# Exact buffers for the probability tiles of a head, GpSimd's running sums gathered in one stretch, the squares of q on ScalarE

## The chip, the cores and the metric

One NeuronCore of a Trainium2 chip runs the whole program. The metric is the device time of one execution in microseconds. All numbers below come from timed runs of the kernel and from one profiled execution of it.

## The reference

A transformer block on x of 2 x 1024 x 256, float32. First attention with 16 heads of 128 (only the part that matters here is shown), then a layer norm over x plus its output, then a mixture of 32 experts with a shared expert, and another layer norm.

```python
q = rmsnorm(q, q_norm_w); k = rmsnorm(k, k_norm_w)      # over the 128 of a head
q = apply_rope(q, cos, sin); k = apply_rope(k, cos, sin)   # the angle depends on the head's index only
scores = jnp.einsum('bhtd,bhsd->bhts', q, k) * scale
scores = 50 * jnp.tanh(scores / 50)
scores = jnp.where(causal_mask, -jnp.inf, scores)
attn = jax.nn.softmax(scores, axis=-1)
out = jnp.einsum('bhts,bhsd->bhtd', attn, v)
return out @ wo.T
```

## The kernel before

**Tiling.** Attention runs in 32 steps `s = 2h + b`, one for each head `h` and batch `b`. In a step the keys of the batch are cut into 8 tiles `j` of 128; tile j holds the transposed probabilities of its 128 keys (partitions) for the queries from 128 j on (columns), so it is 1024, 896, ... 128 columns wide. Float32 accuracy comes from splitting each operand into a "hi" part (rounded to the matmul's format) and a "lo" part (the rest), and from three matmuls hi·hi, lo·hi, hi·lo for each product (`mm3`, L357 to L359). The hi part is made by ScalarE (`copy_hi`, L666), the lo part by VectorE (`lo_of`, L987: source minus hi); q and the weights are split by VectorE alone (a CAST at L997, then the lo).

**A tile's way.** TensorE makes the scores in PSUM; ScalarE takes tanh into `praw` (L699) and exp in place (L705); GpSimd zeroes the upper triangle of the first 128 columns (`mask`, L857); ScalarE makes `prob_hi`, VectorE `prob_lo`; TensorE multiplies with v (`values`). GpSimd also adds every tile to a running sum `pacc` (`accumulate`, L868 and L872), whose column sums TensorE forms with a matmul against ones (`sums`, L391) and which VectorE turns, inverts and uses in the output projection's accumulation (`out_projected`, L1063). Below, "tile j" is VectorE's lo of tile j, and "values j" TensorE's products with it.

**The step's other work.** While a step's scores and values run, the next step's q, k and v are projected, in units that go through two PSUM banks in turn: each unit's matmuls wait until the unit two before has been read out (`open_unit`, semaphore `pj_free`). The order of the units is written out in `UNIT_ORDER` and repeated by hand in the `step` function of each engine: q0, q1, k0, k1 (halves of 512 queries or keys), sums (the column sums of the step before), ss (sums of squares of q and k), four units op0 to op3 of the output projection of the step before, with v0 and v1 between. TensorE's order in a step s (its scores are of s, values 3 to 7 and sums of s-1, the projections for s+1): q0, q1, values 3, scores 0, k0, values 4, k1, scores 1, values 5 to 7, sums, ss, scores 2, scores 3, op0, scores 4, op1, scores 5, v0, op2, values 0 (of s), op3, v1, values 1, scores 6, scores 7, values 2.

**1/rms.** GpSimd squares q (L835) into `qsq`. TensorE sums squares over the head's 128 entries with ones, VectorE turns the result (L1023) into `var`, GpSimd takes the power -1/2 for q (L840) and for k (L843). The one of k is a per-partition scale of the tanh. The one of q must lie along the columns: SP writes it to DRAM (L295) and reads it back as a broadcast to 128 partitions, `rqB` (L297); then VectorE scales q by it (`scale_raw`, L1040) and splits q into `qhat` (cast, lo), which scores 0 of the next step waits for.

**Buffers.** `praw` and `prob` are rings of four tiles of 1024 columns; tanh of tile j waits until tile j-4 has its lo and is added up, and prob_hi of tile j until values j-4 are done. GpSimd's order in a step: masks 6 and 7 and adds 6 and 7 of the step before, squares of q, masks 0 and 1, power for q, adds 0 and 1, masks 2 and 3, add 2, power for k, add 3, and then mask and add of tiles 4 and 5. VectorE's order: (b = 1: split of wo), q0 and q1 out of PSUM, tiles 4 to 7 of the step before, k0 and k1, oT, sums, ss, (b = 0: split of the next q and k weights), op0, tile 0, op1, tile 1, v0, op2, tile 2, op3, scale_raw, tile 3, v1, qhat.

## Time and profile before

| | |
|---|---|
| median of 3 runs | 1169.97 us (1167.75 to 1170.66) |
| the profiled execution | 1168.05 us, its span 1166.3 us |
| busy share of the span: TensorE / VectorE / ScalarE / GpSimd | 88% / 79% / 59% / 68% |
| attention | from the start to about 950 us; the rest is routing and experts |

A busy share is an average over stages; what sets the time of a stage is read from what its engines wait for. A matmul's shown length is longer than its spacing to the next one, since they are pipelined; the spacing counts. In the timeline rows below the first number is the start in us, the second the length in us of the instruction, or of several in a row (x2, x4); an idle time before it and what ended it stand in brackets. Where an engine has to wait after an instruction has begun, for instance to get at the memory, that wait is inside the instruction's length.

### The profile page before, as it was taken

The page shows a single profiled execution, that of the slowest core. Times are in us where ns is not written, and L with a number is a line of the kernel's source. Part 1 is how long each engine was busy: PE and PEld are TensorE (multiplying, and loading weights), DVE is VectorE, ACT ScalarE, POOL GpSimd, SP SyncE. Part 2 cuts the span into 40 slices and gives each one's busy share as a digit, 9 for nine tenths or more (in the row PEclk, how much of TensorE's full clock was granted, in tenths as well). Part 3 has the DMA queues.
Part 4 walks back from the last instruction along what each step waited for, and adds up shares of the span by engine and source line. Part 5 has one row for each costly group of instructions (what it writes and reads, how often), then busy time and mean ns, then how long its engine had stood idle before and what let it go on. Part 6 is the DMA issues. An engine that isn't in the chain of part 4 may idle for free.

```text
span 1166.3 us, 19884 instructions
## 1 busy us (share of the span) xinstructions
PE 1030.0 (88%) x6256; PEld 821.3 (70%) x6256; DVE 922.7 (79%) x1356; ACT 684.7 (59%) x1095; POOL 788.6 (68%) x699
## 2 busy tenths in 40 slices
PE   4799999999999999999999999999999869859910
PEld 3578888888888888878787878787878745335500
DVE  3499999999999999999989899999999885413206
ACT  2476666666666666767676767676767724202303
POOL 1488787878787878787777777777878742262322
PEclk9899999999999999999999999999999989969955
DMA  8110101000001000000000000000000039239435
GB/s 320 46 38 19 38 21 33 23 32 23 32 23 32 23 32 27 27 27 27 27 27 27 27 27 27 27 27 27 27 27 19 19 89 274 54 105 234 86 56 187
DMA packets 49306, 65.97 MB, mean 57 GB/s; under 512 B 10528, under 2 KB 41216, under 8 KB 48768
## 3 DMA queue, kind: packets, MB, share of 16 engines
q1 hardware_dynamic: 43184, 58.55, 16.2%
q0 software_dynamic: 3072, 4.46, 2.2%
q10 hardware_dynamic: 3024, 2.64, 0.7%
q8 instruction: 13, 0.21, 0.1%
q14 instruction: 13, 0.11, 0.0%
HBM read 54.35 MB, written 11.29 MB: 56 GB/s over the span
## 4 chain that ended last, share of the span: by engine, by line
PE 39%; DVE 28%; issue 15%; DMA 9%; ACT 5%; POOL 2%; DVEq 1%; SPq 1%; another core or an unknown queue 0%; ACTq 0%; POOLq 0%
PE ps L357 11%; PE ps L359 10%; PE ps L358 10%; DMA acc_rows<-ye,acci 6%; DVE prob_lo L987 6%; DVE yacc L1063 5%; DVE vS_lo L987 3%; PE ps L385 3%; DVE qhat_hi L997 2%; ACT prob_hi L666 2%; PE ps L391 2%; DVE qhat_lo L987 2%; DVE qraw L1040 2%; PE ps L529 2%; DVE wo_hi L997 1%
## 5 line engine op out<-in xcount | busy, mean ns | idle before, releaser
L987 DVE TENSOR_TENSOR prob_lo<-praw,prob_hi 128x1024 fp32r<-128x1024 f32 (+7 forms) x256 | 370.1, 1474 | 7.3 <-ACT prob_hi L666 7.0
L872 POOL TENSOR_TENSOR pacc<-pacc,praw 128x768 f32<-128x768 f32 (+2 forms) x192 | 268.0, 1396 | 12.8 <-POOL praw L857 9.2
L666 ACT ACTIVATE prob_hi<-praw 128x1024 fp32r<-128x1024 f32 (+7 forms) x256 | 170.8, 681 | 148.5 <-POOL praw L857 147.0
L857 POOL TENSOR_SCALAR_AFFINE_SELECT praw<-praw 128x128 f32<-128x128 f32 x256 | 136.4, 544 | 159.6 <-ACT praw L705 159.6
L699 ACT ACTIVATE praw<-ps,rstd 128x1024 f32<-128x1024 f32 (+7 forms) x256 | 188.2, 736 | 85.0 <-PE ps L359 46.2
L705 ACT ACTIVATE praw<-praw 128x1024 f32<-128x1024 f32 (+7 forms) x256 | 165.6, 672 | 0.0
L357 PE MATMUL ps<-qhat_hi,kT_hi 128*128 128x512 f32 (+3 forms) x384 | 138.6, 361 | 16.6 <-DVE qhat_lo L987 15.7
L357 PE MATMUL ps<-prob_hi,vS_hi 128*128 128x512 f32 (+3 forms) x384 | 136.7, 356 | 4.9 <-DVE prob_lo L987 4.9
L358 PE MATMUL ps<-qhat_lo,kT_hi 128*128 128x512 f32 (+3 forms) x384 | 133.3, 347 | 0.0
L358 PE MATMUL ps<-prob_lo,vS_hi 128*128 128x512 f32 (+3 forms) x384 | 133.3, 347 | 0.0
L359 PE MATMUL ps<-qhat_hi,kT_lo 128*128 128x512 f32 (+3 forms) x384 | 133.2, 347 | 0.0
L359 PE MATMUL ps<-prob_hi,vS_lo 128*128 128x512 f32 (+3 forms) x384 | 132.7, 346 | 0.0
L385 PE MATMUL ps<-wv,xraw 128*128 128x128 f32 x1024 | 126.7, 277 | 0.4 <-DVE kT_lo L987 0.4
L357 PE MATMUL ps<-xT_hi,wqk_hi 128*128 128x512 f32 x256 | 107.3, 419 | 20.7 <-DVE xT_lo L987 12.5
L1063 DVE SCALAR_TENSOR_TENSOR yacc<-ps,rsum,yacc 128x256 f32<-128x256 f32 x256 | 110.9, 473 | 14.2 <-PE ps L359 14.2
L385 PEld LDWEIGHTS ps<-wv,xraw 128*128 128x128 f32 x1024 | 121.1, 192 | 1.2 <-issue 0.8
L357 PEld LDWEIGHTS ps<-qhat_hi,kT_hi 128*128 128x128 f32 x384 | 72.8, 190 | 49.9 <-issue 31.0
L358 PE MATMUL ps<-xT_lo,wqk_hi 128*128 128x512 f32 x256 | 101.8, 398 | 0.0
L359 PE MATMUL ps<-xT_hi,wqk_lo 128*128 128x512 f32 x256 | 101.8, 398 | 0.0
L835 POOL TENSOR_TENSOR qsq<-qraw 128x1024 f32<-128x1024 f32 x32 | 79.3, 2478 | 14.5 <-DVE qraw L1032 14.5
L357 PE MATMUL ps<-wo_hi,oT_hi 128*128 128x256 f32 x256 | 78.8, 308 | 11.5 <-DVE vS_lo L987 7.4
L872 POOL TENSOR_TENSOR pacc<-praw 128x896 f32<-128x896 f32 x32 | 82.2, 2569 | 2.8 <-POOL pacc L868 0.2
(149 smaller groups left out, 2033.4 us busy)
## 6 DMA issues: line engine op xcount, KB each, us to landing
rqB<-rq_rows SPq DMA_DIRECT2D x32, 512.0 KB, 3.7
wgu<-in_wgu SPq DMA_DIRECT2D x16, 704.0 KB
wd<-in_wd SPq DMA_DIRECT2D x16, 352.0 KB
wraw<-in_wqkv SPq DMA_DIRECT2D x16, 256.0 KB, 3.6
acc_rows<-pacc SPq DMA_DIRECT2D x4, 1024.0 KB, 13.4
wv<-in_wqkv SPq DMA_DIRECT2D x16, 128.0 KB, 2.0
woraw<-in_wo SPq DMA_DIRECT2D x16, 128.0 KB, 2.0
yacc<-in_x SPq DMA_DIRECT2D x1, 2048.0 KB, 14.2
```

The costliest lines, as they stand in the source:

```text
L357: mm(out_, left[0], right[0], start=start, stop=False)
L358: mm(out_, left[0], right[1], start=False, stop=False)
L359: return mm(out_, left[1], right[0], start=False, stop=stop)
L385: last = mm(bank[:, P * j:P * j + P], xraw[:, c, t0:t0 + P], wv[:, c, :], start=c == 0, stop=c == KC - 1)
L666: return nc.scalar.activation(dst, src, ACT.Copy)
L699: nc.scalar.activation(praw[:, j % RING, 0:T - P * j], buf[:, P * j:T], ACT.Tanh, scale=rstd[:, b, TT + j:TT + j + 1]).then_inc(tanh_done, 1)
L705: nc.scalar.activation(tile, tile, ACT.Exp, scale=CAP).then_inc(exp_done, 1)
L835: nc.gpsimd.tensor_tensor(qsq[:, :].rearrange("p (g j r) -> p g j r", g=BLK, r=32), q, q, ALU.mult).then_inc(qsq_done, 1)
L857: nc.gpsimd.affine_select(out=diag, in_=diag, compare_op=ALU.is_ge, fill=0.0, base=0, pattern=[[1, P]], channel_multiplier=-1).then_inc(ma ...
L872: nc.gpsimd.tensor_tensor(pacc[:, b, P * j:T], before, raw, ALU.add).then_inc(pacc_done, 1)
L987: v.tensor_tensor(dst, x_, hi.bitcast(F32), ALU.subtract).then_inc(done, 1)
L1063: last = v.scalar_tensor_tensor(y, ps[:, bank_no, D * i:D * i + D], rsum[:, b, 2 * u + i:2 * u + i + 1], y, ALU.mult, ALU.add)
```

## The change

**Buffers.** `RING` becomes 8, and each tile has a region of its exact width in `praw` and `prob`; tile 0 of `praw` has two, for b = 0 and 1. Tanh of tile j now waits for the tile j of the step before to have its lo and to be added, prob_hi for its values. `pacc` holds one step in place of two.

**GpSimd.** All eight adds of a step move behind masks 6 and 7, so into the next step; between the masks stand only the two powers. The squares of q leave GpSimd.

**ScalarE.** It squares q0 and q1 out of PSUM (two instructions of 512 columns) at the head of its step; VectorE's copies of q0 and q1 wait for them. hi 6 moves from the end of a step behind these squares.

**TensorE.** The unit sums moves behind ss, scores 2 and scores 3.

**1/rms of q.** The power is written into a 32-column tile `rq`; VectorE turns it (32 x 32 blocks) behind tile 0, so that SP can write rows of 32 elements, in four DMAs of 8 rows, one for each group of 32 partitions. The broadcast read stays. `rqB` shares its memory with `qsq`, and `sumT` and `rqT` lie in `sqT`.

**Start.** The zeroes for the accumulators in DRAM come out of a buffer of half the size, in 9 DMAs and not 5.

```diff
-RING = 4
+RING = TT
+COLS = [T - P * j for j in range(TT)]
+AT = [sum(COLS[:j]) for j in range(TT)]
+def raw_at(b, j):
+    at = AT[j] if j or not b else sum(COLS)
+    return slice(at, at + COLS[j])
-UNIT_ORDER = "q0 q1 k0 k1 sums ss op0 op1 v0 op2 op3 v1".split()
+UNIT_ORDER = "q0 q1 k0 k1 ss sums op0 op1 v0 op2 op3 v1".split()
...
             def rq_broadcast(step, b):
-                sp.wait_ge(rq_done, step + 1)
-                sp.dma_start(rq_d[b].rearrange("(p j) -> p j", p=P), rstd[:, b, 0:TT]).then_inc(rq_out, 16)
-                sp.wait_ge(rq_out, step * 16 + 16)
+                sp.wait_ge(rqT_done, step + 1)
+                row = rq_d[b].rearrange("(j g r) -> j g r", g=BLK, r=32)
+                for g in range(BLK):
+                    sp.dma_start(row[:, g, :], rqT[32 * g:32 * g + TT, :]).then_inc(rq_out, 16)
+                sp.wait_ge(rq_out, step * 64 + 64)
                 sp.dma_start(rqB[:, :], rq_d[b:b + 1, :].to_broadcast([P, T])).then_inc(rqB_in, 16)
...
             # TensorE's step
                     values(s - 1, 1 - b, 7)
-                    sums(s - 1, 1 - b, *hd.unit(b, "sums"))
                 if new:
                     sums_of_squares(s + 1, *hd.unit(b, "ss"))
                 scores(s, b, 2)
                 scores(s, b, 3)
                 if old:
+                    sums(s - 1, 1 - b, *hd.unit(b, "sums"))
...
             # ScalarE
+                if what[0] == "q":
+                    if not (isinstance(step, int) and step == 0):
+                        act.wait_ge(qf_done, step)
+                    nc.scalar.activation(qsq[:, cols], bank, ACT.Square).then_inc(qsq_done, 1)
+                    return
...
-                act.wait_ge(pacc_done, t + (2 if j == RING else 1))
+                if j:
+                    act.wait_ge(pacc_done, t + 1)
+                elif not (isinstance(s, int) and s == 0):
+                    act.wait_ge(pacc_done, t + 2 - TT)
...
             # ScalarE's step
-                if old:
-                    hi(s - 1, 7)
+                if new:
+                    projected("q0", 1 - b, s + 1, *hd.unit(b, "q0"))
+                    projected("q1", 1 - b, s + 1, *hd.unit(b, "q1"))
+                if old:
+                    hi(s - 1, 1 - b, 6)
+                    hi(s - 1, 1 - b, 7)
                 tanh(s, b, 0)
...
             # GpSimd's step
                 if old:
-                    mask(s - 1, 6)
-                    mask(s - 1, 7)
-                    accumulate(s - 1, 1 - b, 6)
-                    accumulate(s - 1, 1 - b, 7)
-                if new:
-                    square_queries(s + 1, hd.unit(b, "q1")[0])
+                    mask(s - 1, 1 - b, 6)
+                    mask(s - 1, 1 - b, 7)
+                    for j in range(TT):
+                        accumulate(s - 1, 1 - b, j)
+                if new:
                     if b == 1:
                         next_head_weight(h, s)
-                mask(s, 0)
-                mask(s, 1)
+                mask(s, b, 0)
+                mask(s, b, 1)
                 if new:
                     rms_queries(1 - b, hd.unit(b, "ss")[0])
-                accumulate(s, b, 0)
-                accumulate(s, b, 1)
-                mask(s, 2)
-                mask(s, 3)
-                accumulate(s, b, 2)
+                mask(s, b, 2)
+                mask(s, b, 3)
                 if new:
                     rms_keys(1 - b)
-                accumulate(s, b, 3)
-                mask(s, 4)
-                accumulate(s, b, 4)
-                mask(s, 5)
-                accumulate(s, b, 5)
+                mask(s, b, 4)
+                mask(s, b, 5)
...
             # VectorE
+                    dve.wait_ge(qsq_done, step * 2 + int(what[1]) + 1)
                     v.tensor_copy(qraw[:, cols], bank).then_inc(pj_free, 1)
...
+            def turn_rms(step):
+                dve.wait_ge(rq_done, step + 1)
+                v.transpose(rqT[:, :], rq[:, :]).then_inc(rqT_done, 1)
...
                     output_lo(s - 1)
-                    summed(1 - b, *hd.unit(b, "sums"))
                 if new:
                     projected("ss", 1 - b, s + 1, *hd.unit(b, "ss"))
                     if b == 0 and not hd.last:
                         split_next_weights(hd)
                 if old:
+                    summed(1 - b, *hd.unit(b, "sums"))
                     out_projected(1 - b, 0, s - 1, *hd.unit(b, "op0"))
-                tile(s, 0)
+                tile(s, b, 0)
+                if new:
+                    turn_rms(s + 1)
```

## Rows read from the trace of the kernel before

**Rows 1.** The page's first part: busy time of each engine.
```profile
PE 1030.0 (88%) x6256; PEld 821.3 (70%) x6256; DVE 922.7 (79%) x1356; ACT 684.7 (59%) x1095; POOL 788.6 (68%) x699
```
**Rows 2.** Windows: steps A and B; busy time by engine, granted clock, DMA share.
```profile
499.17:528.07 28.90, 27.79 (x177) 23.03 (x177) 27.08 (x34) 19.61 (x31) 22.86 (x20) 1.00 0.08 27
528.07:555.87 27.80, 27.46 (x177) 23.14 (x177) 25.08 (x30) 19.72 (x31) 22.05 (x19) 1.00 0.10 28
```
**Rows 3.** Timeline, TensorE: the matmuls against ones.
```profile
74.70 0.64 PE L391 MATMUL ps<-pacc,ones 128*32 128x256 f32 x8
...
528.53 0.61 PE L391 MATMUL ps<-qsq,ones 128*32 128x256 f32 x8
528.96 0.61 PE L391 MATMUL ps<-ksq,ones 128*32 128x256 f32 x8
529.50 0.38 PE L357 MATMUL ps<-qhat_hi,kT_hi 128*128 128x256 f32 x1
...
895.98 0.64 PE L391 MATMUL ps<-pacc,ones 128*32 128x256 f32 x8
```
**Rows 4.** Timeline, TensorE, steps A and B: matmuls that followed a wait.
```profile
510.00 0.39 PE L357 MATMUL ps<-wo_hi,oT_hi 128*128 128x256 f32 x1 [0.53 <-DVE vS_lo L987]
...
521.99 0.50 PE L357 MATMUL ps<-xT_hi,wqk_hi 128*128 128x512 f32 x1 [0.37 <-DVE qraw L1032]
...
548.49 0.49 PE L357 MATMUL ps<-qhat_hi,kT_hi 128*128 128x512 f32 x1 [0.20 <-DVE qhat_lo L987]
```
**Rows 5.** Timeline, VectorE: step A, and a tile beside an idle GpSimd.
```profile
501.48 0.44 DVE L1073 STREAM_TRANSPOSE sumT<-ps 128x256 f32<-128x256 f32 x1
...
506.75 2.59 DVE L987 TENSOR_TENSOR prob_lo<-praw,prob_hi 128x896 fp32r<-128x896 f32 x1
...
518.63 1.23 DVE L987 TENSOR_TENSOR qhat_lo<-qraw,qhat_hi 128x1024 fp32r<-128x1024 f32 x1
...
522.45 3.86 DVE L987 TENSOR_TENSOR prob_lo<-praw,prob_hi 128x512 fp32r<-128x512 f32 x4
...
930.15 1.07 DVE L987 TENSOR_TENSOR prob_lo<-praw,prob_hi 128x896 fp32r<-128x896 f32 x1
```
**Rows 6.** Timeline, GpSimd: a square at the start, adds of step A.
```profile
19.56 2.07 POOL L835 TENSOR_TENSOR qsq<-qraw 128x1024 f32<-128x1024 f32 x1 [6.09 <-DVE qraw L1032]
...
506.28 2.11 POOL L872 TENSOR_TENSOR pacc<-praw 128x896 f32<-128x896 f32 x1
...
516.75 1.29 POOL L872 TENSOR_TENSOR pacc<-pacc,praw 128x512 f32<-128x512 f32 x1 [0.16 <-POOL praw L857]
...
518.91 1.81 POOL L872 TENSOR_TENSOR pacc<-pacc,praw 128x384 f32<-128x384 f32 x1 [0.16 <-POOL praw L857]
```
**Rows 7.** Timeline, VectorE and GpSimd, end of step B.
```profile
550.19 1.10 DVE L987 TENSOR_TENSOR prob_lo<-praw,prob_hi 128x384 fp32r<-128x384 f32 x1
...
551.82 2.24 DVE L987 TENSOR_TENSOR prob_lo<-praw,prob_hi 128x128 fp32r<-128x128 f32 x1
...
551.57 2.34 POOL L835 TENSOR_TENSOR qsq<-qraw 128x1024 f32<-128x1024 f32 x1
```
**Rows 8.** Groups by line, ScalarE: busy us, mean ns, idle before.
```profile
L683 ACT ACTIVATE ksq<-ps 128x512 f32<-128x512 f32 x64 | 38.1, 596 | 29.7 <-PE ps L359 29.4
```
**Rows 9.** SP's timeline in step A; DMA issues of A, then B, with us to landing.
```profile
504.93 0.32 SPq L295 DMA_DIRECT2D rq_rows<-rstd  x1
506.33 0.32 SPq L297 DMA_DIRECT2D rqB<-rq_rows  x1
...
rqB<-rq_rows SPq DMA_DIRECT2D x1, 512.0 KB, 3.6
...
rqB<-rq_rows SPq DMA_DIRECT2D x1, 512.0 KB, 4.0
```
**Rows 10.** Timeline: VectorE at the start, TensorE and the last attention step.
```profile
36.92 1.28 DVE L1040 SCALAR_TENSOR_TENSOR qraw<-qraw,gcur,rqB 128x1024 f32<-128x1024 f32 x1 [6.94 <-DMA rqB<-rq_rows]
...
945.15 0.55 PE L357 MATMUL ps<-wo_hi,oT_hi 128*128 128x256 f32 x1 [1.90 <-DVE oT_lo L987]
```

138 lines of the change are left out of this document (71 added, 67 removed).

## Prediction

> **What bounds the kernel now.** I began with the page's first part: TensorE is busy for 1030 of 1166 us and VectorE for 923 [rows 1]. Then I looked for the period of the attention loop, the starts of the row-sum matmuls. They alternate between two lengths: step A, in which the next projection weights are split and, near the end, wo, takes 28.90 us, and step B 27.80 us; the clock is full in both [rows 2]. The pattern holds from 74.70 us to 895.98 us, 29 steps of 28.32 us on average [rows 3]. Everything behind the loop, some 220 us, is not touched. So the question is what a pair A+B, now 56.70 us, becomes.
>
> Inside a pair TensorE is the bound, but not alone. In A it sits idle 0.53 us before the output projection that needs v0's bank, and 0.37 before k0, which needs q0's bank; in B 0.20 before scores 0, which needs qhat_lo [rows 4]; A has that one as well, about as long. Around each such wait the starts are some 0.25 us wider apart than those of unbroken matmuls, beyond the idle time itself (the last one's end, the restart), so A loses 0.53 + 0.37 + 0.2 and three times 0.25, 1.9 us, and would take 27.0 without them. B has the same TensorE work, so 27.0 too; its v0 wait is short. All these waits are for VectorE.
>
> VectorE is late because it and GpSimd hold each other up. The lo of tile 1 (896 columns) took 2.59 us; the same shape takes 1.07 when GpSimd is idle. It began at 506.75, GpSimd's 896-column add ran until 508.39, and the rest of the time is the tile's own. In turn GpSimd's 384-column add, begun at 518.91 beside qhat_lo, took 1.81, of which only 0.86 lie behind qhat_lo's end at 519.86 [rows 5, 6]. So they don't share: the one that comes second waits for the whole instruction of the other. Between 550.2 and 554.1 they take turns: tile 7 (128 columns) takes 2.24, until the squares of q are through, and tile 5 1.10 beside a 256-column add [rows 7]. Work of VectorE that reads PSUM (copies of q, kT_lo, yacc) keeps its length.
>
> **The change, part by part.** *The squares of q leave GpSimd*: 2.07 us alone, 2.34 here, once a step [rows 6, 7]. On ScalarE they cost two squares of 0.60, as the squares of k do [rows 8]. ScalarE is busy 19.6 of 28.9 us [rows 2], so this lies beside other work; if that cover were gone, it would be 1.2 us a step. The copy of q waits for them: q1's square ends about 0.7 us behind the projection, at offset 19.6 of the step (offsets count from the step's first row-sum start in the old kernel, and from the end of the values matmuls in the new), while VectorE comes at 18 to 20. Nothing on the path.
>
> *Eight exact buffers and the adds in one stretch*: masks no longer queue behind adds, and tiles 1 to 3 and the cast of q meet only masks (0.29 each). Tile 1 gains 1.5 us in A (2.59 against 1.07), 1.1 in B; tile 2, tile 3 and the cast, each beside an add too, I put at 0.75, 1.35 and 1, their own part taken as 1.2 ns a column from tile 1. The v0 wait of TensorE (0.69, 0.29) goes, and qhat_lo, late now, would be over 2 us early if the rest kept up.
>
> *What is late next: 1/rms of q.* Now GpSimd's power ends at offset 5.7, the first DMA is issued at once, the broadcast 1.40 us behind it, and that lands 3.6 us later in A, 4.0 in B [rows 9]: at 10.8 to 11.0, while VectorE comes at 13.89 (A) and 13.50 (B). Cover: 2.5 to 3.1 us. In the new kernel a 32-column transpose on VectorE stands between; the 256-column one took 0.44 [rows 5], hence about 0.2. It is queued behind tile 0, which ends at 6.9, so it ends at 7.1 (B), 7.25 (A, as the row sums' transpose now stands behind the weight split). Then SP issues four DMAs in place of one: 0.32 each, spaced 0.37, so three more are 1.1 us. With 1.40 from the last issue to the landing, the broadcast starts at 9.65 to 9.8 and lands at 13.4 (A) and 13.65 (B). VectorE, faster by about 2 us up to there, waits 1 to 1.5 us, and scale_raw starts no earlier than now: 0.5 earlier in A, 0.15 later in B. The cover is gone: each further us of this chain is a us of the step. Behind the waiting scale_raw are tile 3, v1's bank, qhat and the q copies. The four writes of 8 rows by 128 B have no row of their own: from below they cost 1.1 us (only issues, if the landings overlap), from above 4.2 (four landings of 1.40 one behind the other, of which one is paid now). I take 1.1: the four are issued without a wait between them, and nothing in rows 9 ties one's landing to the next. The Trainium skill's page "DMA: Bandwidth & Descriptors" (Anatomy of one DMA) gives about 2.0 us as the fixed cost of one DMA on the GpSimd path, where this trace shows 1.40 for the small write; by the page the chain would be 0.6 us longer in each of 29 steps, 17 us, and the total about 1176.
>
> *The stretch of adds meets tiles 4 to 7.* From scale_raw at 13.4 to 13.65: 1.27, tile 3 0.81, v1's lo 0.6, cast 0.6 and a mask 0.3, qhat_lo 1.2: done at 18.1 to 18.3 (now 20.7 and 20.3). ScalarE's exp 7 ends at 17.0, its mask waits for qhat_lo, and the adds start at about 18.9 in B; in A the wo split comes between, 19.5. Uncontended adds: 1024 columns took 2.07 and 384 0.86, 1.9 ns a column between them; the 896- and 512-column rows, 2.11 and 1.29, stand a little above that line [rows 6]. I take 2.0, 1.65, 1.4, 1.2, 0.87, 0.6 and 0.35 for 896 down to 128 columns, with the copy 8.4 in all. By the turns, tile 4 waits for the 896 add, tile 5 for 768, tile 6 for 640, tile 7 for 512: 4.25 us for the last three, 0.65 for tile 4, and 1.97 of their own. Tile 4, wanted at 20.3 (B) or 20.8 (A), so the last is done at 27.15 (B) and 27.75 (A), and k0's lo behind it at 27.8 and 28.4. In the old A they take 3.86 [rows 5]. So of some 4.5 us of contention taken from tiles 1 to 3 and the cast about 3 come back, at the worst place. GpSimd ends its stretch at offset 1.2 of the next step, ahead of mask 0 (2.3) and of the sums (3.3).
>
> *TensorE's order.* The row sums move behind scores 3. Now the three groups of ones-matmuls stand together: the step out of them is 0.54 where inside it is 0.43 [rows 3], and the steps on both sides of that are wider by as much. A group alone pays that again, about 0.3 a step: floor 27.3. Against it stand tile 7 and k0's lo: values 7, the last work of a step, comes 0.35 us before its end and wants tile 7 at 26.95; the sums of squares want k0's bank at 27.3. In A tile 7 is 0.8 late and the bank 1.1, in B 0.2 and 0.5. The two don't add, and the bank's lateness doesn't count in full: VectorE's next chain starts from values 7 (through oT_hi on ScalarE), not from the bank, so the two cycles, TensorE's 27.3 and VectorE's 27.8 (B) or 28.4 (A), meet in turn and the step settles between them, above the tile's 27.5 and 28.1. I take B 27.6, A 28.1. The pair is 55.7, 1.0 us less.
>
> *Ends.* Start-up: VectorE already waits 6.94 us for the first broadcast [rows 10], so the transposes and the three issues, 1.3 us, are paid in full. Tail: two small adds follow the last mask now, and the output projection behind the sums starts at 945.15, after 1.90 us of waiting for oT_lo [rows 10]. The new tail has all eight: masks come sooner, the last at about 937, then 8.4 us and 1.5 of tiles between: sums at 946.9, projection at 947.6, 2.4 later.
>
> Sum: 14.5 pairs x 1.0 = 14.5 us gained, 1.3 and 2.4 lost: 10.8 us. The profiled execution took 1168.05 (span 1166.3), so 1157; it stands 1.9 below the median of 1169.97, hence 1159 for the median.
>
> **Rivals.** *TensorE at its floor*: tiles 4 to 7 don't lose their turns each time, because GpSimd's stretch starts earlier or VectorE gets two turns in a row. For it: ScalarE has slack, and the stretch needs only 8.4 us. Against: in rows 7 no tile gets in ahead of an instruction of GpSimd that is already queued, and in the new order one always is. Pair 54.6, 2.1 x 14.5 = 30.5 less 3.7: 1143. Chance 0.18. *Slower, by the 1/rms chain*: four writes and the broadcast land later than the sum has it. Its place is scale_raw; its price is 29 us for each us, and from 0.4 us more a step the gain is gone. For it: no cover is left, and the writes lengthen from above up to 3.1 us more. Against: of the 1.40 us of the one small write that rows show, 0.32 are the issue, and four issues are in the sum. With 1 us more: 1159 + 29 = 1188. Chance 0.28. *Nothing measurable*: contention only moves, what tiles 1 to 3 gain tiles 4 to 7 give back, 1170: 0.12. The forecast as worked out: 0.42, its own range 1148 to 1166.
>
> **Numbers.** 0.3%, 3.5 us, is about what a measurement tells from no change. Faster: 0.18 and nearly all of 0.42 make 0.57. Same: 0.12 and the edge of the forecast, 0.13. Slower 0.30. The range must hold cases of both signs: it reaches from just below the floor case, 1138, to the 1 us case, 1188; left out, 2 in 10, are a longer chain (the upper bound of 3.1 us would give 1249) and a gain beyond the floor.
>
> **What would show it.** No row for squares on GpSimd; masks at 0.3 us and no wait of prob_hi for them; lo of 896 columns at 1.1, of 384 columns at 2.0 or more; an idle time of VectorE before scale_raw, ended by the broadcast, of 1 to 1.5 us; from first write to broadcast issue 2.5 us; TensorE waiting for tile 7 or kT_lo in place of vS_lo and qraw; pairs of 55.7. Wrong if scale_raw waits well over 1 us (slower), or if the stretch of adds lies ahead of tile 4 (faster).

## The result, and the profile after

The changed kernel takes 1137.02 us (median of 4 runs, 1134.95 to 1139.3), the one before on the same chip 1169.88 (4 runs, 1167.75 to 1170.66): a ratio of 0.9722, 95% interval 0.970 to 0.9745. It is faster, by 32.9 us. The forecast was 1159 us, 10.8 us faster, and the measurement lies 1 us below its range. Of the four executions of the kernel four_waits (below) two, the profiled one among them, were of a slower kind with a lower clock; its time below is that of the other two, and its rows are read for their order.

The first lines are the page's busy time by engine (it answers to [rows 1]) and the shares by engine of the chain that ended last; then come two steps of the loop, in the windows' columns as in [rows 2], each cut 0.23 us ahead of k's group of the sums of squares.

```profile
PE 1009.9 (89%) x6256; PEld 821.5 (72%) x6256; DVE 843.9 (74%) x1388; ACT 701.5 (62%) x1159; POOL 634.0 (56%) x668
...
PE 75%; DMA 11%; DVE 6%; issue 3%; POOL 2%; ACT 1%; SPq 1%; POOLq 0%; ACTq 0%; DVEq 0%
```
```profile
515.04:542.00 26.96, 26.96 (x180) 23.13 (x176) 22.47 (x32) 20.15 (x34) 17.80 (x20) 1.00 0.08 29
542.00:568.96 26.96, 26.96 (x180) 23.13 (x176) 24.18 (x35) 20.15 (x34) 17.31 (x18) 1.00 0.10 29
```

The chain runs over TensorE for 75% of the span, where it was 39% in the kernel before. VectorE has lost 79 us of busy time though nothing but a few small transposes was added to it and no arithmetic taken away. What is gone is time spent waiting for GpSimd inside instructions: the lo of tile 1 takes 1.08 us where it took 2.59. Both kinds of step take 26.96 us, and in both TensorE is busy from end to end at the full clock (granted 1.00, which is 2.4 GHz); a pair is 53.92 us where it was 56.70. TensorE's timeline shows where that pace begins and ends: the first two row sums, the k half of the sums of squares of four steps, and the last row sums.

```profile
81.23 0.64 PE L406 MATMUL ps<-pacc,ones 128*32 128x256 f32 x8
110.82 0.61 PE L406 MATMUL ps<-ksq,ones 128*32 128x256 f32 x8
113.64 0.64 PE L406 MATMUL ps<-pacc,ones 128*32 128x256 f32 x8
137.78 0.61 PE L406 MATMUL ps<-ksq,ones 128*32 128x256 f32 x8
...
542.23 0.61 PE L406 MATMUL ps<-ksq,ones 128*32 128x256 f32 x8
...
865.75 0.61 PE L406 MATMUL ps<-ksq,ones 128*32 128x256 f32 x8
...
915.83 1.08 PE L406 MATMUL ps<-pacc,ones 128*32 128x256 f32 x8 [7.03 <-POOL pacc L894]
```

The same groups of the kernel before began at 103.27 and 896.87. So the 28.8 us by which the span is shorter (1166.3 against 1137.5) divide as follows. Up to 103.27 or 110.82: 7.6 us lost. From there 28 steps: 793.6 against 754.9, 38.7 us gained. Behind 896.87 or 865.75: 269.4 against 271.8, 2.3 us lost.

VectorE's and GpSimd's timelines at the end of a steady step, where the forecast had its trouble:

```profile
527.75 1.28 DVE L1062 SCALAR_TENSOR_TENSOR qraw<-qraw,gcur,qsq 128x1024 f32<-128x1024 f32 x1 [0.60 <-DMA qsq<-rq_rows]
528.95 0.82 DVE L1002 TENSOR_TENSOR prob_lo<-praw,prob_hi 128x640 fp32r<-128x640 f32 x1
...
530.29 0.68 DVE L1012 CAST qhat_hi<-qraw 128x1024 fp32r<-128x1024 f32 x1
531.00 1.22 DVE L1002 TENSOR_TENSOR qhat_lo<-qraw,qhat_hi 128x1024 fp32r<-128x1024 f32 x1
533.04 0.69 DVE L1050 COPY qraw<-ps 128x512 f32<-128x512 f32 x1 [0.82 <-ACT qsq L699]
534.32 0.69 DVE L1050 COPY qraw<-ps 128x512 f32<-128x512 f32 x1 [0.59 <-ACT qsq L699]
534.93 5.83 DVE L1002 TENSOR_TENSOR prob_lo<-praw,prob_hi 128x512 fp32r<-128x512 f32 x4
540.68 1.27 DVE L1002 TENSOR_TENSOR kT_lo<-ps,kT_hi 128x512 fp32r<-128x512 f32 x2
```
```profile
531.02 1.60 POOL L877 TENSOR_SCALAR_AFFINE_SELECT praw<-praw 128x128 f32<-128x128 f32 x2 [3.25 <-ACT praw L728]
532.58 0.29 POOL L890 COPY pacc<-praw 128x128 f32<-128x128 f32 x1
532.95 2.13 POOL L894 TENSOR_TENSOR pacc<-praw 128x896 f32<-128x896 f32 x1
535.16 7.36 POOL L894 TENSOR_TENSOR pacc<-pacc,praw 128x768 f32<-128x768 f32 x5
```

Read it in this order. The scaling of q waits 0.60 us for the broadcast, so the chain of 1/rms has no cover, as forecast. The cast and qhat_lo have their own lengths, since no add is under way. The copies of q read PSUM and keep 0.69 us beside the 896-column add. Tiles 4 to 7 then take 5.83 us for some 2 us of work: tile 4 comes ahead of the 768-column add and takes 0.70, and tiles 5, 6 and 7 stand behind the adds of 768, 640 and 512 columns (2.20, 1.78 and 1.38 us). The lo of k0 is the first of two in 1.27 us, so its bank is free at about 541.3; the sums of squares, which need it, start at 541.77. The turns are there, and k0's bank is free in time, by 0.4 us (0.2 in the steps with wo's split, where the bank is free at about 568.5 and its group starts at 568.73).

### The profile page after: what moved, and what is told of

Same layout as the page of the kernel before. It is cut to its first block, busy times and chain, and to the rows that moved or that the text cites. A ratio compares the mean times of both kernels' runs of the same rounds, so it can differ in the third digit from the quotient of the medians.

```text
span 1137.5 us, 20522 instructions
## 1 busy us (share of the span) xinstructions
PE 1009.9 (89%) x6256; PEld 821.5 (72%) x6256; DVE 843.9 (74%) x1388; ACT 701.5 (62%) x1159; POOL 634.0 (56%) x668
## 4 chain that ended last, share of the span: by engine, by line
PE 75%; DMA 11%; DVE 6%; issue 3%; POOL 2%; ACT 1%; SPq 1%; POOLq 0%; ACTq 0%; DVEq 0%
PE ps L372 20%; PE ps L373 19%; PE ps L374 19%; PE ps L400 9%; DMA acc_rows<-ye,acci 7%; PE ps L406 4%; PE ps L544 2%; DMA qsq<-rq_rows 1%; DMA yacc<-in_x 1%; DVE prob_lo L1002 1%; POOL pacc L894 1%; PE ps L554 1%; DVE qhat_lo L1002 1%; POOL xg L980 1%; POOL lnr L990 1%
## 5 line engine op out<-in xcount | busy, mean ns | idle before, releaser
L1002 DVE TENSOR_TENSOR prob_lo<-praw,prob_hi 128x1024 fp32r<-128x1024 f32 (+7 forms) x256 | 313.6, 1253 | 3.1 <-ACT prob_hi L681 3.1
L877 POOL TENSOR_SCALAR_AFFINE_SELECT praw<-praw 128x128 f32<-128x128 f32 x256 | 120.2, 471 | 306.5 <-ACT praw L728 288.9
L894 POOL TENSOR_TENSOR pacc<-pacc,praw 128x768 f32<-128x768 f32 (+2 forms) x192 | 241.7, 1259 | 16.6
L722 ACT ACTIVATE praw<-ps,rk 128x1024 f32<-128x1024 f32 (+7 forms) x256 | 185.9, 740 | 86.9 <-PE ps L374 82.8
L681 ACT ACTIVATE prob_hi<-praw 128x1024 fp32r<-128x1024 f32 (+7 forms) x256 | 168.0, 683 | 1.3 <-POOL praw L877 1.3
L372 PE MATMUL ps<-qhat_hi,kT_hi 128*128 128x512 f32 (+3 forms) x384 | 136.0, 354 | 13.7 <-DVE qhat_lo L1002 13.3
L372 PE MATMUL ps<-xT_hi,wqk_hi 128*128 128x512 f32 x256 | 102.0, 398 | 18.1 <-DVE xT_lo L1002 12.2
L374 PE MATMUL ps<-xT_hi,wqk_lo 128*128 128x512 f32 x256 | 101.4, 396 | 0.0
L372 PEld LDWEIGHTS ps<-prob_hi,vS_hi 128*128 128x128 f32 x384 | 72.7, 189 | 11.2 <-DVE prob_lo L1002 6.0
L374 PEld LDWEIGHTS ps<-qhat_hi,kT_lo 128*128 128x128 f32 x384 | 73.3, 191 | 8.6
```

What stands on the lines that cost most here:

```text
L372: mm(out_, left[0], right[0], start=start, stop=False)
L374: return mm(out_, left[1], right[0], start=False, stop=stop)
L681: return nc.scalar.activation(dst, src, ACT.Copy)
L722: nc.scalar.activation(praw[:, raw_at(b, j)], buf[:, P * j:T], ACT.Tanh, scale=rk[:, b, j:j + 1]).then_inc(tanh_done, 1)
L877: nc.gpsimd.affine_select(out=diag, in_=diag, compare_op=ALU.is_ge, fill=0.0, base=0, pattern=[[1, P]], channel_multiplier=-1).then_inc(ma ...
L894: nc.gpsimd.tensor_tensor(pacc[:, P * j:T], before, raw, ALU.add).then_inc(pacc_done, 1)
```

## The experiments

Ratios are to the kernel before, on the same chip; intervals are 95%. A step is the mean of 22 steady steps, from one k group of the sums of squares to that 22 steps later. "Scaling" is the start of the scaling of q, "q's hat" the end of qhat_lo, both as means of these steps, counted from that group's start. The times of different kernels come in part from different chips; where two ratios lie close, the steps tell more than the totals.

| kernel | us | ratio, interval | step | scaling | q's hat |
|---|---|---|---|---|---|
| before | 1167 to 1170 | 1 | 28.34 | 12.81 | 19.60 |
| after | 1137.0 | 0.972, 0.970 to 0.975 | 26.96 | 12.63 | 17.12 |
| q_squares_alone | 1205.6 | 1.033, 1.028 to 1.038 | 29.47 | 12.80 | 19.60 |
| squares_on_gpsimd | 1242.8 | 1.062, 1.057 to 1.067 | 30.65 | 15.57 | 20.09 |
| adds_in_turn | 1208.9 | 1.033, 1.028 to 1.038 | 29.49 | 12.64 | 18.95 |
| eight_buffers | 1175.7 | 1.007, 1.005 to 1.010 | 28.22 | 12.61 | 18.94 |
| one_add_a_mask | 1214.3 | 1.041, 1.039 to 1.043 | 29.63 | 12.59 | 20.17 |
| two_waits | 1151.1 | 0.988, 0.984 to 0.992 | 27.36 | 13.33 | 17.85 |
| four_waits | 1325.5 | 1.137, 1.132 to 1.143 | 33.83 | 15.10 | 23.09 |
| short_adds | 1118.7 | 0.960, 0.956 to 0.964 | 26.96 | 12.63 | 17.14 |
| one_write | 1133.0 | 0.970, 0.965 to 0.974 | 27.14 | 11.79 | 16.27 |
| one_write_hold | 1127.5 | 0.967, 0.964 to 0.970 | 26.96 | 11.79 | 16.26 |
| hold_and_tail | 1124.6 | 0.962, 0.960 to 0.964 | 26.96 | 11.79 | 16.27 |

### The parts one by one

**q_squares_alone**: the old kernel with the squares moved.

```diff
+                if what[0] == "q":     # ScalarE
+                    squares_free(step)
+                    turned = qsq[:, cols].rearrange("p (g j r) -> p g j r", j=TT, r=32)
+                    nc.scalar.activation(turned, bank.rearrange("p (g r j) -> p g j r", r=32, j=TT), ACT.Square).then_inc(qsq_done, 1)
+                    return
...
+                    dve.wait_ge(qsq_done, step * 2 + int(what[1]) + 1)
                     v.tensor_copy(qraw[:, cols], bank).then_inc(pj_free, 1)
...
-                    square_queries(s + 1, hd.unit(b, "q1")[0])
```

> The kernel before with one part of the change: the squares of q are taken by ScalarE from the bank, four buffers and the adds between the masks stay. Theory (a steady step is bound by the turns that VectorE and GpSimd take at its end, and 2.1 to 2.3 us of squares are one of the turns there): the end of a step comes some 0.5 us earlier and 28 steps give 10 to 18 us, 1150 to 1160 us; TensorE's steps stay above the 26.96 us of the changed kernel, since the adds of tiles 6 and 7 and of tiles 0 to 5 still stand among VectorE's own work. Rival 1 (the squares were the whole of it): 1137 to 1143 us, and steps of 26.96 us. Rival 2 (only the adds' place or the buffers count): 1166 to 1172 us.

Measured: 37.5 us slower. All three expectations were wrong, the sign too. ScalarE's timeline shows why:

```profile
567.42 0.63 ACT L666 ACTIVATE prob_hi<-praw 128x512 fp32r<-128x512 f32 x1 [1.69 <-POOL praw L856]
...
569.58 0.53 ACT L666 ACTIVATE prob_hi<-praw 128x384 fp32r<-128x384 f32 x1 [0.96 <-POOL praw L856]
...
571.80 0.42 ACT L666 ACTIVATE prob_hi<-praw 128x256 fp32r<-128x256 f32 x1 [1.50 <-POOL praw L856]
572.30 1.09 ACT L684 ACTIVATE qsq<-ps 128x512 f32<-128x512 f32 x2
```

What stands behind the squares, on VectorE and TensorE:

```profile
572.93 1.29 DVE L1031 COPY qraw<-ps 128x512 f32<-128x512 f32 x2 [2.28 <-ACT qsq L684]
573.68 0.50 PE L357 MATMUL ps<-xT_hi,wqk_hi 128*128 128x512 f32 x1 [1.24 <-DVE qraw L1031]
```

The hi parts wait for masks, and the masks stand behind adds on GpSimd. Those waits are in the kernel before too (1.70, 0.96 and 1.50 us in its timeline) and cost little there. Now the squares are queued behind them, and the copy of q, which opens q's bank for k, waits for the squares: 2.28 us in this step, and TensorE 1.24 us for that copy.

**adds_in_turn**: the changed kernel with each add in its own step again.

```diff
-                    for j in range(TT):
-                        accumulate(s - 1, 1 - b, j)
+                    accumulate(s - 1, 1 - b, 6)
+                    accumulate(s - 1, 1 - b, 7)
...
                 mask(s, b, 3)
+                accumulate(s, b, 0)
+                accumulate(s, b, 1)
+                accumulate(s, b, 2)
                 if new:
                     rms_keys(1 - b)
+                accumulate(s, b, 3)
                 mask(s, b, 4)
+                accumulate(s, b, 4)
                 mask(s, b, 5)
+                accumulate(s, b, 5)
```

> The changed kernel with one part undone: GpSimd adds each tile in its own step again, between the masks (tiles 0 to 2 after the four masks, 3 to 5 one by one, 6 and 7 in the next step), not in one stretch; eight buffers, the squares on ScalarE and the turned 1/rms stay. Theory (what counts is that no adds meet tiles 0 to 3, the cast and the rest of q's hat, which stand on the way to the next scores): the adds of tiles 0 to 3 (some 6.5 us of GpSimd) meet them again, and a step takes 27.3 to 28.0 us: 1145 to 1165 us. Rival 1 (the squares and the buffers did it, the place of the adds is free as long as a step has room): 1128 to 1138 us, since the start-up and the tail, where the stretch is late, get their 8 us back. Rival 2 (the place is all of the gain): 1165 to 1172 us.

Measured: 72 us slower than the changed kernel, beyond all three. The step is within 0.02 us of that of q_squares_alone, and it has the same wait, longer:

```profile
567.57 0.63 ACT L681 ACTIVATE prob_hi<-praw 128x512 fp32r<-128x512 f32 x1 [4.35 <-POOL praw L877]
...
568.42 0.35 ACT L722 ACTIVATE praw<-ps,rk 128x128 f32<-128x128 f32 x1
...
569.88 1.06 ACT L699 ACTIVATE qsq<-ps 128x512 f32<-128x512 f32 x2
```

Tanh 7 and the squares both start late, so TensorE waits for a scores buffer (33 us in the run) and for the copies of q (27 us), by the view of waits. What the two kernels share is the pairing: squares on ScalarE, and masks behind adds. That their steps agree to 0.02 us may be chance, since part of TensorE's waits differ (here the scores buffer, in q_squares_alone the banks of q, of v0 and q's hat); eight_buffers below tests the pairing.

**squares_on_gpsimd**: the changed kernel with the squares back.

```diff
                     mask(s - 1, 1 - b, 7)
+                if new:
+                    square_queries(s + 1, hd.unit(b, "q1")[0])
+                if old:
                     for j in range(TT):
                         accumulate(s - 1, 1 - b, j)
```

> The changed kernel with one part undone: the squares of q are again GpSimd's (2.1 us, read from the copy in SBUF), between the masks of tiles 6 and 7 and the stretch of adds; eight buffers, the stretch and the turned 1/rms stay. Theory (turns): 2.1 us more of GpSimd's work stands ahead of the adds in the stretch in which VectorE needs its tiles 4 to 7, whose last now ends 0.4 us before TensorE needs k0's bank; at most one turn of some 2 us is put in, so k0 comes up to 1.6 us late in each of 29 steps: 1160 to 1185 us. Rival (the squares run beside the copies of q, which read PSUM and take no turn, and cost nothing): 1135 to 1141 us.

Measured: 106 us slower, far beyond the theory, and of another cause. GpSimd's timeline, then TensorE's:

```profile
558.17 2.27 POOL L855 TENSOR_TENSOR qsq<-qraw 128x1024 f32<-128x1024 f32 x1 [2.03 <-DVE qraw L1052]
560.39 0.62 POOL L890 COPY pacc<-praw 128x128 f32<-128x128 f32 x1
561.09 2.17 POOL L894 TENSOR_TENSOR pacc<-praw 128x896 f32<-128x896 f32 x1
563.34 7.29 POOL L894 TENSOR_TENSOR pacc<-pacc,praw 128x768 f32<-128x768 f32 x6
570.58 0.19 POOL L899 COPY gcur<-ghead 128x1 f32 x1
570.71 0.54 POOL L877 TENSOR_SCALAR_AFFINE_SELECT praw<-praw 128x128 f32<-128x128 f32 x2
571.22 1.65 POOL L860 TENSOR_TENSOR rq<-var,mhalf 128x8 f32<-128x8 f32 x1
```
```profile
570.69 0.64 PE L406 MATMUL ps<-pacc,ones 128*32 128x256 f32 x8 [1.87 <-POOL pacc L894]
```

GpSimd first waits 2.03 us for both copies of q, and the whole stretch moves back behind the squares. It then ends in the next step, where the row sums wait for it (73.5 us in the run, all but 7 of it in the loop), and masks 0 and 1 and 1/rms of q stand behind it, so the scaling of q comes 2.9 us later. TensorE's granted clock falls too: in each step it is 0.5 (1.2 GHz) for 3.4 us, behind the idle time before the row sums (that ends at 570.69, the clock falls at 571.6), 0.944 as a mean over the loop. A step of 30.65 us at 0.944 has lost about 1.7 us to it, by an estimate from these numbers, of the 3.7 us by which it is longer; the rest is the wait.

**eight_buffers**: squares on GpSimd and adds in turn, the rest as changed (the diffs of both kernels above, with the squares behind adds 6 and 7).

> The changed kernel with both parts on GpSimd undone: squares of q on GpSimd, adds between the masks of their own step; the eight buffers, the turned 1/rms and the sums behind the scores stay. It completes a square: both parts 1137 us, squares on ScalarE alone 1209 us, the stretch alone 1243 us. Theory (each part alone puts work on a chain that the other one keeps free; without both, VectorE copies q from its bank without waiting for ScalarE, and the stretch is not there to delay the masks): near the kernel before, 1160 to 1185 us, so the two parts interact and their single prices do not add. Rival (the prices add: 1137 + 72 + 106): 1290 to 1330 us.

Measured: 1175.7, as the theory has it, and not near the sum of the two prices. The 4.36 us wait of a hi part for its mask is here as well, and TensorE waits about a microsecond a step for the scores buffer (34 us in the run), but the copies of q don't wait for ScalarE. So the buffers, with the turned 1/rms and the moved row sums, bring next to nothing: the step is 28.22 where it was 28.34. From there the squares on ScalarE alone make it 1.3 us longer, the stretch alone 2.4, and both together 1.3 shorter. What the moved row sums do by themselves was not tried.

**one_add_a_mask**: the stretch begun earlier.

```diff
                 mask(s, b, 4)
+                accumulate(s, b, 0)
                 mask(s, b, 5)
+                accumulate(s, b, 1)
...
                     mask(s - 1, 1 - b, 6)
+                    accumulate(s - 1, 1 - b, 2)
                     mask(s - 1, 1 - b, 7)
-                    for j in range(TT):
+                    for j in range(3, TT):
```

> The changed kernel with the stretch of adds begun earlier: add 0 behind the mask of tile 4, add 1 behind that of tile 5, add 2 behind that of tile 6, the other five behind that of tile 7, so that no mask has more than one add ahead of it. It takes the kernel adds_in_turn apart, where three to four adds and 1/rms of k stand ahead of the mask of tile 4 and ScalarE waits 4.35 us for that mask. Theory A (what costs there is the masks that stand behind adds, and through them ScalarE and its squares of q): one add of 2.1 us ahead of tile 6's mask costs little, steps of 26.96 to 27.5 us, 1130 to 1150 us. Theory B (adds 0 and 1 now meet the cast and the rest of q's hat, as in the third step of the changed kernel, and make q's hat late): steps of 28 to 30 us, 1165 to 1215 us.

Measured: 1214.3, theory B. ScalarE no longer waits for masks (5.6 us in the run, 163 in adds_in_turn). The adds now meet VectorE's own chain: the scaling of q takes 2.91 us in place of 1.28, the cast 1.98, and q's hat ends 3.05 us later than in the changed kernel. In steps with wo's split that is caught as well (1.66 and 1.44 us for 0.38 and 0.43), and those take 30.5 us and more, up to 32.1 where the granted clock is 0.95. So it isn't enough that masks come in time. The stretch has to lie behind the last mask and behind q's hat too.

### The price of the 1/rms chain

**two_waits** and **four_waits** lengthen the chain.

```diff
                     sp.dma_start(row[:, g, :], rqT[32 * g:32 * g + TT, :]).then_inc(rq_out, 16)
+                    if g in (1,):        # four_waits: (0, 1, 2)
+                        sp.wait_ge(rq_out, step * 64 + 16 * g + 16)
```

> The changed kernel with its 1/rms chain made longer by one wait: SyncE waits for the first two of its four writes of a step before it issues the other two. By the changed kernel's rows a write lands 1.4 us after its issue, so the broadcast is issued some 1.4 us later than the 2.20 us measured behind the first write. Theory A (the sum of the prediction: every us of the chain beyond the slack of 0.4 us, which tile 7 and k0's bank have, costs all 29 steps a us): 29 x 1.0 = 29 us, 1162 to 1172 us. Theory B (the turns amplify: the cast and the rest of q's hat then meet the adds of 2.1 and 2.2 us, as they do in the second step of the changed kernel): 1.4 us of delay become 2.5 to 4 us, 1190 to 1240 us. Rival (the chain has slack that the prediction did not see, a steady step is TensorE's): 1136 to 1145 us, with steps of 26.96 us still.

> The changed kernel with a wait behind each of the four writes of 1/rms, so that they go one after another: about 1.75 us each in place of 2.20 us for all, the broadcast some 4.5 us later. Theory A (a us of the chain beyond 0.4 us costs 29 us): 1137 + 29 x 4.1 = 1250 to 1265 us. Theory B (the turns amplify at first, but a delay of 4.5 us takes the cast and the rest past most of the adds, so that not more than one turn is lost on top): 1260 to 1320 us. Rival (slack): below 1180 us.

Measured: the broadcast is issued 3.0 us behind the first write in two_waits and 4.62 in four_waits, against 2.20; both expectations had taken a write that is waited for as slower than it is. Two_waits scales q 0.70 us later and its step is 0.40 longer; its 1151.1 us lie in none of the three ranges. A slack of 0.3 us and a us for each us beyond it would give this, but one point can't show such a rule. The timelines have turns in it: in most steps the 896-column add begins 0.5 us later and tile 4 now waits for it (1.2 to 1.5 us where it takes 0.7 to 1.0), for steps of 27.2 to 27.5; and at 346.96 wo's lo begins 0.1 us behind that add and takes 2.30 us for 0.43, in a step of 28.3. Four_waits scales q 2.47 us later and its step is 6.87 longer. A step on VectorE, then GpSimd:

```profile
401.32 1.28 DVE L1064 SCALAR_TENSOR_TENSOR qraw<-qraw,gcur,qsq 128x1024 f32<-128x1024 f32 x1 [3.22 <-DMA qsq<-rq_rows]
...
403.96 2.62 DVE L1014 CAST qhat_hi<-qraw 128x1024 fp32r<-128x1024 f32 x1
406.61 2.71 DVE L1004 TENSOR_TENSOR qhat_lo<-qraw,qhat_hi 128x1024 fp32r<-128x1024 f32 x1
409.24 1.64 DVE L1014 CAST wo_hi<-woraw 128x256 fp32r<-128x256 f32 x1
410.92 1.44 DVE L1004 TENSOR_TENSOR wo_lo<-woraw,wo_hi 128x256 fp32r<-128x256 f32 x1
```
```profile
403.54 0.29 POOL L892 COPY pacc<-praw 128x128 f32<-128x128 f32 x1
403.91 2.12 POOL L896 TENSOR_TENSOR pacc<-praw 128x896 f32<-128x896 f32 x1
```

The cast starts 0.05 us behind the 896-column add and loses its turn, and so does each instruction behind it, with an add of its own: 3.4 us on the way to q's hat, then 2.3 more in wo's split. TensorE's granted clock is 0.95 and 0.90 in the two steps around this stretch, 0.933 over the loop; a step of 33.83 us at 0.933 has lost some 2.3 us to it (an estimate from these two numbers), so about 4.6 of the 6.87 are waits. Theory B's amplification is small in two_waits, where the cast is nearly always still ahead of the adds, and in four_waits it is more than the one turn that B allowed, so that B's 1260 to 1320 us was a little low (1321.8 and 1329.2). What decides is which of the two engines is first at that one place.

### The floor, the start and the tail

**short_adds** leaves the adds out but for 8 columns each, so its output is not the block's; `pacc` is filled with a constant once, at the start.

```diff
+                    few = slice(P * j, P * j + 8)
+                    before = praw[:, raw_at(b, 0)][:, few] if j == 1 else pacc[:, few]
-                    nc.gpsimd.tensor_tensor(pacc[:, P * j:T], before, raw, ALU.add).then_inc(pacc_done, 1)
+                    nc.gpsimd.tensor_tensor(pacc[:, few], before, raw[:, 0:8], ALU.add).then_inc(pacc_done, 1)
```

> The changed kernel with each add of the running sums cut to 8 columns (the sums are then those of a few columns only, over a large constant, and the output isn't the reference's). Theory (the steady steps are TensorE's, the adds cost only in the start-up and at the tail): steps stay 26.96 us; the second and third step lose the 2.8 and 7.5 us less, and the sums behind the last step need not wait 7 us for the adds: 1117 to 1125 us. Rival (the adds still hold up every step a little): steps below 26.9 us and under 1112 us.

Measured: 1118.7, steps of 26.96 to the hundredth. The theory holds. So 26.96 us is TensorE's, and the adds cost the changed kernel nothing in a steady step. All of their price (18 us by the medians, 20.6 by the profiled spans) is at the ends: the fourth sums of squares come at 100.45 in place of 110.82, and the last two intervals between row sums are 20.88 and 14.97 us in place of 25.75 and 21.52. What the adds do at the start is this, in the changed kernel's second step, on VectorE and GpSimd:

```profile
93.22 1.28 DVE L1062 SCALAR_TENSOR_TENSOR qraw<-qraw,gcur,qsq 128x1024 f32<-128x1024 f32 x1 [2.86 <-DMA qsq<-rq_rows]
...
95.86 2.62 DVE L1012 CAST qhat_hi<-qraw 128x1024 fp32r<-128x1024 f32 x1
98.51 2.71 DVE L1002 TENSOR_TENSOR qhat_lo<-qraw,qhat_hi 128x1024 fp32r<-128x1024 f32 x1
```
```profile
95.81 2.12 POOL L894 TENSOR_TENSOR pacc<-praw 128x896 f32<-128x896 f32 x1
```

It is four_waits' pattern: here the writes and the broadcast alone took 2.2 us longer than in a steady step (3.03 us to the broadcast's issue, and a later landing), and VectorE lost 3.4 us more to the adds. The clock is in the price too: TensorE's granted clock is 0.5 from 70.9 to 74.3 and from 101.6 to 105.0, each time behind waits (2.60 us for a copy of q from 67.7 on, 2.68 us for qhat_lo from 98.7 on), and 1.00 throughout these steps in short_adds and in the kernel before. Two times 3.4 us at half the clock are up to 3.4 us, an estimate from these rows.

**one_write** takes the chain's three extra writes away.

```diff
-                    nc.scalar.activation(qsq[:, cols], bank, ACT.Square).then_inc(qsq_done, 1)
+                    turned = qsq[:, cols].rearrange("p (g j r) -> p g j r", j=TT, r=32)
+                    nc.scalar.activation(turned, bank.rearrange("p (g r j) -> p g j r", r=32, j=TT), ACT.Square).then_inc(qsq_done, 1)
...
-                for g in range(BLK):
-                    sp.dma_start(row[:, g, :], rqT[32 * g:32 * g + TT, :]).then_inc(rq_out, 16)
+                sp.dma_start(rq_d[b].rearrange("(p j) -> p j", p=P), rq[:, 0:TT]).then_inc(rq_out, 16)
...
-                    turn_rms(s + 1)
```

> The changed kernel with the 1/rms of q written by one transfer as before: ScalarE writes the squares in the order of the old layout (reading the bank with a stride), VectorE turns nothing, SyncE issues one write of 128 short rows and then the broadcast. Theory: the chain to the scaling of q gets 0.5 to 1 us shorter (three issues and the turn go, a write of more and shorter rows comes back); the steady steps stay at TensorE's 26.96 us, and the start-up, where the chain is late and the rest of q's hat then meets the adds, gets 2 to 6 us back: 1131 to 1135 us. Rival 1 (the strided squares take longer than 0.60 us each and hold up the copies of q and with them the tiles): 1138 to 1150 us. Rival 2 (no change): 1136 to 1139 us.

Measured: 1133.0, inside the theory's range, but by two misses that cancel in part. The squares with a stride take 0.60 us as before, the scaling of q starts 0.84 us earlier and VectorE no longer waits for it. The start-up gives back 12 us (the second row sums at 101.2 in place of 113.6), where 2 to 6 were expected, but every second step now takes 27.32 us and not 26.96. The ratios of this kernel and of the changed one have intervals that overlap, so the two differences are shown by the traces and not by the totals. VectorE and GpSimd at the end of such a step:

```profile
524.41 0.69 DVE L1049 COPY qraw<-ps 128x512 f32<-128x512 f32 x1 [0.59 <-ACT qsq L698]
525.02 6.47 DVE L1001 TENSOR_TENSOR prob_lo<-praw,prob_hi 128x512 fp32r<-128x512 f32 x4
```
```profile
522.60 2.12 POOL L893 TENSOR_TENSOR pacc<-praw 128x896 f32<-128x896 f32 x1
524.80 7.91 POOL L893 TENSOR_TENSOR pacc<-pacc,praw 128x768 f32<-128x768 f32 x6
```

An earlier stretch is a worse one: the second add begins at 524.80, 0.2 us ahead of tile 4, and the tiles stand behind four whole adds.

**one_write_hold** gives tile 4 the first turn.

```diff
+                    if j == 2:
+                        pool.wait_ge(plo_done, s * TT + 4 + 1 + RING)
                     pool.wait_ge(pacc_done, t + RING)
                     nc.gpsimd.tensor_tensor(pacc[:, P * j:T], before, raw, ALU.add).then_inc(pacc_done, 1)
```

> The kernel one_write (squares in the old order, one write of 1/rms) with one wait more on GpSimd: the add of tile 2 (768 columns) starts only when VectorE has done tile 4 of the same old step. In one_write every second step takes 27.33 us and not 26.96, and there tile 4 starts 0.2 us behind that add and waits for it, so that tile 7 stands behind four adds and k0's bank is 0.3 us late. Theory (turns): with tile 4 first, tile 7 stands behind three adds, every step is 26.96 us, and 14 or 15 x 0.37 = 5 us come back: 1125 to 1129 us. Rival 1 (the turn falls to the add anyway before tile 5, and the adds only end later): 1131 to 1138 us. Rival 2 (later adds hold up the masks and 1/rms of the next step): over 1138 us.

Measured: 1127.5, all steps 26.96, as the theory has it. The total alone wouldn't tell it from one_write's (0.964 to 0.970 against 0.965 to 0.974); the steps do.

```profile
522.70 4.71 DVE L1003 TENSOR_TENSOR prob_lo<-praw,prob_hi 128x512 fp32r<-128x512 f32 x4
```
```profile
520.28 2.12 POOL L895 TENSOR_TENSOR pacc<-praw 128x896 f32<-128x896 f32 x1
523.54 7.63 POOL L895 TENSOR_TENSOR pacc<-pacc,praw 128x768 f32<-128x768 f32 x6 [1.15 <-DVE prob_lo L1003]
```

GpSimd waits 1.15 us, the four tiles take 4.71 us in place of 6.47, and the stretch still ends before GpSimd is wanted again.

**hold_and_tail** adds, in the last step only, between the masks.

```diff
+                if not new:
+                    accumulate(s, b, 0, qsq)
+                    accumulate(s, b, 1, qsq)
+                    mask(s, b, 2)
+                    mask(s, b, 3)
+                    accumulate(s, b, 2, qsq)
+                    mask(s, b, 4)
+                    accumulate(s, b, 3, qsq)
+                    mask(s, b, 5)
+                    accumulate(s, b, 4, qsq)
+                    return
```

> The kernel one_write_hold with one edit more: in the last step, which has no next one beside it, GpSimd adds tiles 0 to 4 between its masks, into the free buffer of the squares, and only tiles 5 to 7 are left behind the last mask. In one_write_hold the ones matmuls of the last sums wait 7.0 us for those adds, and GpSimd is idle for 7 us of the last step. Theory: the adds end before the last values, the wait goes, the last interval between sums is 15 us in place of 21.3: 1120 to 1123 us. Rival (a mask behind an add makes a tile late in that step, and the values lose what the sums win): 1123 to 1128 us.

Measured: 1124.6 (5 runs, 1119.17 to 1126.0), in the rival's range, and the trace has both. The 7.0 us wait of the last sums is gone, but the last interval is 16.8 us where 15 was expected and 21.5 measured without the edit: the lo of tiles 1 and 2 take 2.47 and 1.79 us beside adds, and the values end 2.5 us later. It has the lowest time of the kernels that leave nothing out, 3.8% under the kernel before and about 1% under the changed one. The two comparisons with and without the edit are from different chips, and their intervals touch, so that this edit makes the kernel faster isn't shown clear of noise.

## Why the forecast was wrong

**What bounds, and the contention.** Right. In these traces VectorE's casts and subtractions that read SBUF take whole turns with GpSimd's adds (cast 2.62 us for 0.68), and its copies from PSUM don't (0.69). The waits for v0's bank and the slow cast are gone, and ScalarE's hi parts waited 1.3 us for masks in the whole run, 147 before. Single masks still lose a turn, as the one at 531.02 behind qhat_lo (1.36 us for 0.29), at no cost.

**Squares on ScalarE, "nothing on the path".** Right for the whole change, and wrong for its reason. The forecast looked at ScalarE's busy share and at when the squares end. What keeps the squares off the path is that no hi part ahead of them waits for a mask, and that comes from the stretch: q_squares_alone and adds_in_turn show 1.1 to 1.3 us more a step where it is missing. The forecast didn't see that the two parts need each other, though the waits of prob_hi for masks stood in the trace of before.

**The 1/rms chain.** Nearly right. Transpose 0.20, first write to broadcast issue 2.20 where 2.5 was forecast, the issues 0.33 apart where 0.37 was, VectorE's wait 0.4 to 1.0 where 1 to 1.5 was. The scaling starts 13.1 us behind the values' end as a mean (12.63 behind k's group, which starts 0.46 behind q's group and so behind the values), where 13.4 and 13.65 were forecast. The lower bound of the four writes, 1.1 us, was the right one. The price, "29 us for each us", was too high for a small amount (0.40 us a step for 0.70, two_waits) and far too low past the start of the adds (6.87 for 2.47, the lower clock included, four_waits).

**The step that failed: "The stretch of adds meets tiles 4 to 7", and the pair of 55.7 us that came of it.** The mechanism was right, down to which tile stands behind which add. The size was off, by small amounts that nearly all pointed one way. In B tile 4 starts 20.1 us behind the values' end where 20.3 was forecast, and the four tiles take 5.83 us where 6.87 was the sum: tile 4 takes 0.70 us, with nothing of the 0.65 that it was to wait for the 896-column add, and the other three take 5.13 where about 5.5 was meant. That add is all but over when tile 4 comes: q's hat ends at 17.6 as a mean and not at 18.1 to 18.3, so that it begins at 18.1 and not at 18.9 (B). A stretch that lies ahead of tile 4 was the forecast's own sign of being wrong on the fast side, and its first long add does. In A tile 4 starts at 20.1 too and not at 20.8, since wo's split lies in the wait for the squares, and the four take 6.04. So k0's lo ends at 26.55 (B) and 26.77 (A) and not at 27.8 and 28.4, and its bank is free 0.4 and 0.2 us ahead of its use, where 0.5 and 1.1 behind was forecast. On the other side the floor is 26.96 and not 27.3: for the lone group of ones matmuls 0.3 us was put, and it doesn't show. One term erred the other way and did no harm: the stretch takes 10.5 us and not 8.4, but as it begins earlier it ends at 1.3 (B) and 1.5 (A) of the next step, where 1.2 was forecast.

A sum that ends within a microsecond of a floor should have given the floor more than 0.18. The measured pair of 53.9 is that rival's outcome and below its 54.6. Half of its reason is what happened, since the stretch does start earlier; but tiles 5 to 7 lose their turns all the same, and only tile 4 hardly does. The argument against it ("no tile gets in ahead of an instruction of GpSimd that is already queued") was beside the point: the tiles lose their turns and are still in time.

**Start-up.** Forecast 1.3 us, measured 7.6. The transposes and issues were counted, the amplification not: a step whose 1/rms is 2 us late pays up to 3.4 more, because the cast then falls behind the first long add, and the waits for it are followed by 3.4 us at half the clock, twice. Short_adds, in which that can't happen, has the fourth sums of squares 2.8 us ahead of the kernel before.

**Tail.** Forecast 2.4 us, measured 2.3.

**Sum.** By the forecast's terms: 14.5 us gained in the loop, 1.3 and 2.4 lost. Measured: 38.7, 7.6 and 2.3. Two errors cancel in part: the loop gained 24 us more than forecast and the start-up lost 6 more, so the miss of the whole (28.8 us by the profiled spans for 10.8) is smaller than that of the term that failed.

What stays open: in the second step the four writes take 3.03 us to the broadcast's issue (3.21 in short_adds) and not 2.20, and the broadcast lands 1.3 us later than elsewhere. One_write has its usual 1.4 us in that step, and 3.38 in the third. The traces have one thing beside it. In those of all 13 kernels together, this interval is longer than the kernel's usual one in ten steps (by 0.2 to 2.0 us), and in each of the ten a DMA packet of the kind "instruction" starts inside it (in the changed kernel at 86.73, 8 KB); of the other steps one has such a packet there (four_waits, at 162.48) and isn't late. Ten of ten is hard to call chance, but no run shows that the packet is the cause, and for the late landing nothing is shown.

## What to carry to other kernels

Where two engines exclude each other for whole instructions, work out which of them is first at each meeting, and by how much: here 0.2 us in who came first at tile 4 cost 0.4 us in every second step, and a chain 2.5 us later cost 6.9 in each, a part of it through TensorE's clock. A long unsplit stretch of the second engine belongs behind the last of its short instructions that others wait for, and beside those of the first engine that read PSUM; a single wait can hand the first turn to the engine that is on the path. Price the parts of such a change together: here the squares on ScalarE alone lost 33 us against neither part, the stretch alone 67, and both together won 39.

## What the runs showed of the hardware

A one-input cast from SBUF to SBUF waits for GpSimd too: 128x1024 took 2.62 us beside a GpSimd add and 0.68 alone. A 128x512 copy from PSUM to SBUF took 0.69 us beside the 896-column add. The Trainium skill's page "SBUF — State Buffer" (SBUF: two separate sides) has a lock of the port pair that VectorE and GpSimd share, held for a whole instruction by whichever of the two starts first. The trace agrees: the 2.62 us of the cast at 403.96 end 0.55 us behind the add that had begun 0.05 us ahead of it.

A write of 1/rms to DRAM that SyncE waits for (8 rows of 128 B) takes 1.15 us from issue to the next: four_waits' four need 4.62. Issued without a wait, four need 2.20 to the broadcast's issue. One write of 128 rows of 32 B needs 1.40.

ScalarE reads a PSUM bank with a stride of 8 columns as fast as without one: the square of 128x512 took 0.60 us both ways.

TensorE's granted clock fell to 0.5 (1.2 GHz) for 3.4 us behind a wait of 1.87 us (squares_on_gpsimd, wait until 570.69, fall at 571.6) and of 2.68 us (the changed kernel, until 101.4 and at 101.6). It stayed at 1.00 in the steady steps of q_squares_alone, whose longest wait is 1.26 us.
